# Score matmuls of 48 and 49 rows in two halves of the partitions, with the heads of a pair stacked above each other

## The reference

```
D = E // H                      # 16 numbers a head
qh = q.reshape(B, S, KV, G, D).transpose(0, 2, 3, 1, 4)
kh = k.reshape(B, S, KV, D).transpose(0, 2, 1, 3)
scores = einsum('bkgsd,bktd->bkgst', qh, kh) / 4
weights = softmax(scores, axis=-1)
out = einsum('bkgst,bktd->bkgsd', weights, vh)
```

## Time and profile before

| | us |
|---|---|
| median of 3 runs | 2073.77 |
| range of the runs | 2072.3 to 2074.99 |
| span of the profiled execution | 2071.6 |
| VectorE busy in the span | 1417.0 (68%) |
| TensorE busy in the span | 1536.0 (74%) |
| ScalarE busy in the span | 717.8 (35%) |

### The profile page before, as it was taken

How to read it: one execution, slowest core, us unless ns; L and a number is a source line. 1 busy time by engine, 2 the same in 40 slices (tenths; PEclk the granted TensorE clock), 3 DMA queues, 4 the chain that set the end, 5 groups by cost and what they waited for, 6 DMA issues and landing times.

```text
span 2071.6 us, 25320 instructions
## 1 busy us (share of the span) xinstructions
PE 1536.0 (74%) x8378; PEld 759.6 (37%) x8379; DVE 1417.0 (68%) x2322; ACT 717.8 (35%) x976; POOL 414.0 (20%) x318
## 2 busy tenths in 40 slices
PE   2121313069993899992589888898889999999997
PEld 1111212046662566661122222222234444444443
DVE  7999999963336222227988787888656777777765
ACT  2134342521122233333166565665612222222221
POOL 3054443410000111115200000000022222222222
PEclk7565655579996999996599999999989999999999
DMA  5223231310013122225502011020300000000000
GB/s 185 81 102 125 85 96 64 124 44 24 20 48 103 61 81 81 81 76 145 170 1 39 14 21 32 0 46 21 130 13 1 0 20 0 20 0 0 20 0 21
DMA packets 54861, 113.90 MB, mean 55 GB/s; under 512 B 8520, under 2 KB 24136, under 8 KB 51728
## 3 DMA queue, kind: packets, MB, share of 16 engines
q1 hardware_dynamic: 49040, 94.29, 14.2%
q0 software_dynamic: 5760, 18.88, 3.4%
HBM read 72.11 MB, written 31.46 MB: 50 GB/s over the span
## 4 chain that ended last, share of the span: by engine, by line
PE 39%; DVE 29%; issue 19%; POOL 7%; ACT 3%; DMA 2%; DVEq 0%; SPq 0%; POOLq 0%; ACTq 0%
PE PS L635 13%; PE PS L650 7%; PE PS L1360 5%; DVE WORK L1485 5%; PE PS L1339 5%; DVE BIG L1659 4%; POOL BIG L1664 3%; PE PS L1348 3%; DVE BIG L1658 2%; DVE BIG L1660 2%; POOL BIG L1668 2%; ACT BIG L1672 2%; PE PS L625 1%; DVE WORK L1658 1%; DMA WORK<-in_L_ffn_w_dram 1%
## 5 line engine op out<-in xcount | busy, mean ns | idle before, releaser
L1485 DVE TENSOR_REDUCE WORK<-PS 128x1 f32<-128x512 f32 x512 | 326.3, 685 | 71.3 <-PE PS L1339 68.4
L1870 PE MATMUL PS<-BIG 128*128 128x512 f16 x1536 | 339.8, 383 | 8.6 <-DVE BIG L1941 6.8
L1267 ACT ACTIVATE BIG<-PS 128x1024 f32<-128x1024 f32 x256 | 261.5, 1024 | 165.8 <-PE PS L1348 164.6
L635 PE MATMUL PS<-BIG,WORK 128*128 (+1 forms) x1728 | 273.7, 316 | 5.1 <-DVE WORK L670 4.7
L1339 PE MATMUL PS<-BIG 128*128 128x512 f16 x512 | 205.6, 404 | 68.9 <-DVE WORK L1485 45.1
L1870 PEld LDWEIGHTS PS<-BIG 128*128 128x128 f16 x1536 | 151.3, 99 | 194.4 <-issue 14.3
L635 PEld LDWEIGHTS PS<-BIG,WORK 128*128 128x128 f16 x1728 | 168.1, 99 | 97.7 <-issue 12.7
L1893 PE MATMUL PS<-BIG 128*128 128x512 f16 x768 | 175.7, 382 | 16.3 <-DVE BIG L1965 16.3
L674 DVE SCALAR_TENSOR_TENSOR WORK<-PS,WORK 128x352 f32<-128x352 f32 x72 | 37.7, 524 | 211.7 <-ACT WORK L662 211.7
L1348 PE MATMUL PS<-BIG 128*128 128x512 f16 x512 | 155.2, 387 | 0.1
L650 PE MATMUL PS<-BIG,WORK 128*128 (+1 forms) x648 | 151.7, 379 | 3.8 <-DVE WORK L679 3.8
(11 more groups left out here) (225 smaller groups left out, 2265.2 us busy)
## 6 DMA issues: line engine op xcount, KB each, us to landing
wdq_scratch<-BIG SPq DMA_DIRECT2D x12, 1024.0 KB, 4.8
BIG<-wdq_scratch SPq DMA_DIRECT2D x12, 1024.0 KB, 6.1
WORK<-in_L_ffn_w_dram SPq DMA_DIRECT2D x32, 352.0 KB, 3.8
y_scratch<-WORK SPq DMA_DIRECT2D x40, 256.0 KB, 2.5
BIG<-BIG SPq DMA_DIRECT2D x96, 64.0 KB, 2.3
BIG<-in_L_ffn_gate_w_dram SPq DMA_DIRECT2D x4, 1024.0 KB, 6.3
BIG<-in_L_ffn_up_w_dram SPq DMA_DIRECT2D x4, 1024.0 KB, 7.4
X<-in_x_dram SPq DMA_DIRECT2D x4, 1024.0 KB, 14.0
```

Of the source, the lines that this page charges most:

```text
L635: ins = nc.tensor.matmul(bank[1 + 2 * m + up][:, 0:I], xT[:, p, a, k * P:(k + 1) * P], W13[:, bass.ds(slot * W13N + (w * half + k * 2 * I ...
L1267: nc.scalar.activation(PB[:, tp, 2 * h:2 * h + 2, :], BPAIR[h % 2], ACT.Exp, scale=SOFT_SCALE).then_inc(exp_ok, 1)
L1485: v.tensor_reduce(MXU[:, g % 2, c:c + 1], ABANK[i], AX_X, ALU.max, negate=True).then_inc(max_ok, 1)
L1870: ins = nc.tensor.matmul(bank[b], fxT[:, p, a, k * P:(k + 1) * P], w[:, c, l, k, :], start=(i == 0), stop=(i == 3 * KD - 1))
```

## The change

Two heads of a group now stand in the two halves of the partitions: the 48 rows of the even heads in 0 to 47, those of the odd heads in 64 to 111. QS has half as many columns (H/2 instead of H heads), and KK is written to both halves, in one copy instead of two. The maxima go to rows 48 and 112, in two DMAs. An A matmul uses 48 rows of one half, a B matmul 49. Each is issued as a matmul on 64 of the array's 128 rows: rows 0 to 63 or rows 64 to 127. The order in a slot is A (lower half), B (upper), B (lower), A (upper). B matmuls signal one by one. The stacking of one group takes 12 DMAs instead of 6. The clearing of the unused rows goes: VectorE, GpSimd and ScalarE cleared whole ranges before the stage, and VectorE wrote the row of ones (L1559); now GpSimd and VectorE fill 32 rows of KK each with ones. The order of the UW weight loads at the end of the stage is another, as the columns come free in another order.

```diff
-                    sp.dma_start(QS[rows, g * HG:(g + 1) * HG, :], qhT[g * HD:(g + 1) * HD, a, :, :]).then_inc(qk_in[g], 16)
-                    sp.dma_start(KK[rows, g, :, :], khT[g * HD:(g + 1) * HD, w, :].unsqueeze(1).to_broadcast([HD, 2, S])
-                                 ).then_inc(qk_in[g], 16)
+                    for i in range(2):
+                        rows = slice(64 * i + n * HD, 64 * i + (n + 1) * HD)
+                        sp.dma_start(QS[rows, g * HP:(g + 1) * HP, :], heads[g * HD:(g + 1) * HD, a, :, i, :]
+                                     ).then_inc(qk_in[g], 16)
+                        sp.dma_start(KK[rows, g, :], khT[g * HD:(g + 1) * HD, w, :]).then_inc(qk_in[g], 16)
...
-                sp.dma_start(QS[64:65, g * HG:(g + 1) * HG, :].rearrange("o h (r s) -> o (h r) s", r=R),
-                             MT[:, i, :]).then_inc(m_in[i], 16)
+                for half in range(2):
+                    row = 64 * half + ROWS
+                    sp.dma_start(QS[row:row + 1, g * HP:(g + 1) * HP, :].rearrange("o h (r s) -> o (h r) s", r=R),
+                                 MT[half * HP * R:(half + 1) * HP * R, i, :]).then_inc(m_in[i], 16)
...
-                    r = 2 * tp + i
-                    nc.tensor.matmul(ABANK[i], QS[:, g * HG + h, r * P:(r + 1) * P], KA[:, g, :],
+                    r = 2 * tp + h // 2
+                    rows = slice(64 * i, 64 * i + ROWS)
+                    nc.tensor.matmul(ABANK[i], QS[rows, g * HP + h % 2, r * P:(r + 1) * P], KK[rows, g, :],
                                      start=True, stop=True).then_inc(a_mm, 1)
...
-                for j in range(HALF):
-                    t = HALF * tp + j
-                    ins = nc.tensor.matmul(BPAIR[h % 2][:, j, :], KS[:, g, t * P:(t + 1) * P],
-                                           QS[:, g * HG + h, :], start=True, stop=True)
-                ins.then_inc(b_mm, 1)
+                t = HALF * tp + h // 2
+                for i in (1, 0):
+                    rows = slice(64 * i, 64 * i + ROWS + 1)
+                    nc.tensor.matmul(BPAIR[h % 2][:, i, :], KK[rows, g, t * P:(t + 1) * P],
+                                     QS[rows, g * HP + h % 2, :], start=True, stop=True).then_inc(b_mm, 1)
...
-            link(v.memset(QS.rearrange("p a b -> p (a b)")[32:64, :].bitcast(F32), 0.0))
+            v.memset(KK.rearrange("p a b -> p (a b)")[96:128, :].bitcast(F32), ONE_ONE).then_inc(ones_ok, 1)
...
-            v.memset(KS[64:65, :, :], 1.0).then_inc(cpad_ok, 1)
```

More of the change, by code:

```diff
@@ L1 @@
+import struct
 from contextlib import ExitStack
@@ L739, in b_gpsimd @@
             pool.wait_ge(MO.y_mm, SLOTS)
[L740 removed]
+            nc.gpsimd.memset(KK.rearrange("p a b -> p (a b)")[32:64, :].bitcast(F32), ONE_ONE).then_inc(ones_ok, 1)
             for p in range(2):
@@ L1085, in build @@
         HG = H // G
[L1086 to L1089, removed]
+        HP = HG // 2
+        ROWS = 3 * HD
+        QS = carve(BIG, "QS", 0, [P, H // 2, S], F16)
+        KK = carve(BIG, "KK", 32768, [P, G, S], F16)
+        ONE_ONE = struct.unpack("<f", struct.pack("<I", 0x3C003C00))[0]
         PB = carve(BIG, "PB", 49152, [P, 2, 2 * HG, S])
@@ L1108, in build @@
         ct_in = sem("ct_in")
-        cpad_ok = sem("cpad_ok")
-        zeros_ok = sem("zeros_ok")
+        ones_ok = sem("ones_ok")
         row_st = sem("row_st")
@@ L1162, in stack_group @@
             def stack_group(b, g):
+                heads = qhT.rearrange("p a (h i) s -> p a h i s", i=2)
                 for n, (a, w) in enumerate(((0, 0), (0, 1), (1, 0))):
-                    rows = slice(n * HD, (n + 1) * HD)
-                    sp.dma_start(QS[rows, g * HG:(g + 1) * HG, :], qhT[g * HD:(g + 1) * HD, a, :, :]).then_inc(qk_in[g], 16)
-                    sp.dma_start(KK[rows, g, :, :], khT[g * HD:(g + 1) * HD, w, :].unsqueeze(1).to_broadcast([HD, 2, S])
-                                 ).then_inc(qk_in[g], 16)
+                    for i in range(2):
[3 more added lines that the diff above has]
+                        sp.dma_start(KK[rows, g, :], khT[g * HD:(g + 1) * HD, w, :]).then_inc(qk_in[g], 16)
             def maxima(u, g, i):
                 sp.wait_ge(mt_ok, u + 1)
-                sp.dma_start(QS[64:65, g * HG:(g + 1) * HG, :].rearrange("o h (r s) -> o (h r) s", r=R),
-                             MT[:, i, :]).then_inc(m_in[i], 16)
+                for half in range(2):
+                    row = 64 * half + ROWS
+                    sp.dma_start(QS[row:row + 1, g * HP:(g + 1) * HP, :].rearrange("o h (r s) -> o (h r) s", r=R),
+                                 MT[half * HP * R:(half + 1) * HP * R, i, :]).then_inc(m_in[i], 16)
             def batch(b, last):
@@ L1183, in batch @@
                         maxima(u + 1, (g + 1) % G, (g + 1) % 2)
[L1184 to L1188, removed]
+                    if last and g == 2:
+                        load_weights(UW, 1, 2, uw_in)
+                    if last and g == 4:
+                        sp.wait_ge(b_mm, u * 4 * HG)
+                        load_weights(UW, 1, 0, uw_in)
+                    if last and g == 6:
+                        load_weights(UW, 1, 3, uw_in)
                     if last or g < 5:
@@ L1193, in batch @@
                     for gg in {5: (0, 1, 2, 3), 6: (4, 5), 7: (6,)}[g]:
-                        sp.wait_ge(b_mm, (b * G + gg + 1) * 2 * HG)
+                        sp.wait_ge(b_mm, (b * G + gg + 1) * 4 * HG)
                         stack_group(b + 1, gg)
                 if not last:
-                    sp.wait_ge(b_mm, (b * G + G) * 2 * HG)
+                    sp.wait_ge(b_mm, (b * G + G) * 4 * HG)
                     stack_group(b + 1, G - 1)
@@ L1204, in c_sync @@
             load_ctx(0)
-            sp.wait_ge(cpad_ok, 1)
+            sp.wait_ge(ones_ok, 2)
             sp.wait_ge(t_free, tuse(None, "q", R - 1) + 1)
@@ L1215, in c_sync @@
             batch(B - 1, True)
-            sp.wait_ge(b_mm, B * G * 2 * HG)
-            load_weights(UW, 1, FCH - 1, uw_in)
+            sp.wait_ge(b_mm, B * G * 4 * HG)
+            load_weights(UW, 1, 1, uw_in)
             sp.wait_ge(pv_mm, B * G * 2)
@@ L1265, in batch @@
                         for h in range(HG):
-                            act.wait_ge(b_mm, n * HG + (h + 1))
+                            act.wait_ge(b_mm, n * (2 * HG) + 2 * (h + 1))
                             nc.scalar.activation(PB[:, tp, 2 * h:2 * h + 2, :], BPAIR[h % 2], ACT.Exp,
@@ L1283, in c_scalar @@
             act.wait_ge(MO.y_mm, SLOTS)
[L1284 to L1287, removed]
             nc.scalar.nop().then_inc(exp_ok, 2)
@@ L1359, in pv @@
                 for h in range(HG):
-                    ins = nc.tensor.matmul(OBANK[32 * h:32 * h + 32, :], V[:, t, g, :], PB[:, tp, 2 * h + j, :],
+                    ins = nc.tensor.matmul(OBANK[32 * h:32 * h + 32, :], V[:, t, g, :], PB[:, tp, HG * j + h, :],
                                            start=(t == 0), stop=(t == R - 1))
@@ L1370, in batch @@
                         if tp == 0:
-                            pe.wait_ge(m_in[g % 2], (u - g % 2) * 8 + 16)
+                            pe.wait_ge(m_in[g % 2], (u - g % 2) * 16 + 32)
                         ahead = not (last and g >= G - 2)
@@ L1483, in max_slot @@
                     dve.wait_ge(a_mm, n + 1)
-                    c = h * R + 2 * tp + i
+                    c = i * HP * R + h % 2 * R + 2 * tp + h // 2
                     v.tensor_reduce(MXU[:, g % 2, c:c + 1], ABANK[i], AX_X, ALU.max, negate=True).then_inc(max_ok, 1)
```

9 lines of the change are left out of this document (3 added, 6 removed).

## The result

| | before | after |
|---|---|---|
| median, us | 2074.38 (4 runs, 2072.3 to 2075.64) | 2181.2 (4 runs, 2172.56 to 2183.26) |
| span of the profiled execution | 2071.6 | 2178.3 |
| TensorE clock over the span | 0.872 | 0.826 |

The account below looks back on a forecast made before the run. Bound by the turn between TensorE and VectorE, neither full, with SyncE's queue as third party. 2071.6 + 20.9 prologue + 54.3 boundaries + 3 clock - 7.5 overlap = 2142.3; median 2.2 higher, 2144.5 us, range 2105 to 2158.

Parts of the forecast that it names:

- the clock's 3: TensorE behind long stalls at the three batch boundaries: half clock for a few us, 1 us each, 3 us lost.
- The issue doesn't shrink with the size: SyncE's stacking DMAs: half-size transfers keep the present issue pitch, about 0.655 us, 0.685 in the prologue.
- rival (a): SyncE's queue: issue time goes with size, pitch 0.33 us, nothing stalls, 2065 us; chance 0.05.
- rival (b): SyncE's queue: small transfers issue somewhat faster, at 0.545 us, 2107 us; chance 0.20.
- the prologue: Start of the stage: 96 stacking DMAs instead of 48 delay unit 0's first maxima, costing 20.9 us.
- The stalls: Three batch boundaries: TensorE waits for SyncE's transfers before groups 6, 7 and next group 0, not group 1; 18.1 us each.
- the queue's terms: SyncE's doubled issues at the start and three batch boundaries: 20.9 us plus 54.3 us lost.
- The halves overlap: TensorE's A and B matmuls in alternating halves run side by side: 0.27 us a unit, 7.5 us gained in all.
- rival (c): TensorE's score matmuls: the halves don't overlap, no 7.5 us gained, 2152 us, or 2158 with pitch 0.685; chance 0.15.
- The drain between tilings: TensorE's tiling mode changes: some 0.1 us each, 6 to 10 us if all on the chain; put at 0.

Follow-up runs that it names:

- queue-only kernel: Kernel before, full 128-row matmuls, with every stacking DMA and the maxima's DMA split in two; 2146.3 us, ratio 1.0358.
- experiment 6: Changed kernel with every score matmul on all 64 rows of its half, the added rows zeros against ones; 2151.36 us, ratio 1.0381.
- Experiment 3: Changed kernel with every B matmul issued twice, 2166.54 us; also with SyncE's transfers spread, 2103.73; then context load moved, B twice only in groups 0 to 4, 2101.7.
- experiment 7: Changed kernel, KK stacking by GpSimd, all 64 rows: 2074.66 us; plus B twice in groups 0 to 4: 2078.08; control, kernel before with spread transfers: 2072.99.
- experiment 5: Kernel before with score matmuls on 48 or 49 rows of one half, one after the other, on 64 array rows; 2305.46 us, ratio 1.1133.

## Why the prediction was wrong, point by point

Distances between the maxima's transposes (of units counted from 0), each less that of before, in us; 1 is the queue-only kernel, 6 the one on 64 rows:

| stretch | predicted | after | 1 | 6 |
|---|---|---|---|---|
| start to unit 0 | 20.9 | 17.0 | 18.4 | 18.5 |
| units 0 to 5 | -1.4 | 9.3 | 0.1 | 1.2 |
| boundary, 5 to 9 | 18.6 | 22.5 | 19.7 | 21.8 |
| units 9 to 13 | -1.1 | 8.2 | 0.1 | -0.4 |
| boundary, 13 to 17 | 18.6 | 20.9 | 16.5 | 18.3 |
| units 17 to 21 | -1.1 | 8.1 | -0.1 | 0.5 |
| boundary, 21 to 25 | 18.6 | 23.6 | 17.6 | 20.5 |
| units 25 to 30 | -2.4 | 0.0 | -0.1 | -1.8 |

The predicted column shares out the 70.7 us of the sum, with the clock's 3 in the boundaries (18.1 + 1 less 0.5 for two units). The after column sums to 109.6; the span grew by 106.7, so 2.9 are gained outside these stretches. Of the 36.7 us between the forecast and the result, the clock is most (below).

**The issue doesn't shrink with the size: right.** 591 and 627 ns against the earlier trace rows; rival (a) would have had 0.33 us, rival (b) 0.545. The prologue's pitch was 0.661 (0.685 taken) and the first issue came 1.05 us earlier, so the first slot of unit 0 starts at 1045.19 and not at 1048.4, and the prologue cost 17.0, not 20.9; the boundaries' pitch was 0.671 ((1167.75 - 1135.55) / 48), not 0.655.

**The stalls: right in size, not in every place.** At the first boundary TensorE waits 3.04 us before group 6 for a stack (3.7 forecast) and 11.49 before group 7 (some 11 named). Before the next group 0 it waits 1.43 and not 3 to 4, for group 7 had run in part at half clock and ended later. Before group 1 it waits 5.97 where the forecast had "no further stall"; the queue-only kernel waits 3.88 there, so this slip is not the clock's. In that kernel the start and the three boundaries cost 72.2 us together (18.4 + 19.7 + 16.5 + 17.6), where 20.9 + 54.3 = 75.2 were forecast, and 78.2 with the clock's 3: the queue's terms hold, and the clock behind stalls alone was not put too low.

**The halves overlap: right.** 13.33 us a unit; rival (c) falls. Units with the transposes of q, 14.61 us before, take 14.20 where the clock holds (experiment 6), so these gain 0.4 and not 0.27. The drain between tilings, put at 0, has no visible price: the chain is as forecast, and from the last A matmul to the PV block it is 0.31 us (1545.38 to 1545.69) as before.

**The clock, "behind long stalls the clock is at half for a few us: 1 us each, 3": this step failed.** The sum took the full clock of the earlier trace rows as given for the new matmuls, and charged only the stalls. The fewer rows also take from TensorE what kept its clock up: it ran at half clock in large parts of units that wait for no transfer. That the halved time does so too fits experiments 3 and 6, but no run isolates it. Experiment 6 measures the term by giving the rows back: 2181.2 - 2151.4 = 29.8 us instead of 3, and rather more, since its own clock is not full everywhere. Without it the forecast is 2141.5, and 2151.4 was measured. By the table, the boundaries are 7.8 of the difference (60.6 against 52.8 without the clock) and the units between them 5.5 (-0.5 against -6.0, for the first units of a batch are still at a clock share below 1 in experiment 6), less 2.4 in the prologue; that is 10.9 for a difference of 9.9, and the rest is rounding and what lies outside the table's stretches.

**What is shown and what is open.** Rows were changed both ways, and the clock moved with them each time. From 48 or 49 to 64 in each half, nothing else in the form of the matmuls changed (experiment 6, faster by 30, and in experiment 7 faster by 35). From 128 to 48 or 49 (experiment 5, slower by 233), the part of the array that a matmul is issued on went from 128 rows to 64 as well; how much of the 233 is due to that, no run shows. Experiment 3 moved the clock with more work on the same rows. Not settled: whether rows of zeros count as much as rows of data (they do count), why the last batch of the changed kernel keeps the full clock with the same forms of matmuls, and why three or four units of experiment 5 do.

## What to carry to other kernels

- Before matmuls are made narrower in rows, read the granted clock of the stage, and price the stage at both clocks: at 1.2 GHz the PV block cost 1.86 instead of 0.99 us. If the clock falls, fill the rows: on a half's 64 rows the matmuls cost no time more than on 48 (13.33 us a unit both times), and zeros in one of the two operands were enough here.
- A queue that binds nothing has slack, not no cost: count its issues (0.59 to 0.63 us each on SyncE, from 2 KB to 64 KB) between two transfers that somebody waits for. Moving half of them to GpSimd, with the rows filled, brought the changed kernel from 2181 to 2075, level with before. Its units away from the boundaries do gain what the halves gave (most take 14.20 and 13.33 us against 14.61 and 13.61), but its start costs 3.5 us more, and in the first units of a batch the clock is still not full.

## What the runs showed of the hardware that was not expected

- TensorE busy 50.00 of 50 us at a granted clock of 0.50 (matmuls on 48 or 49 rows), and at 1.00 when busy 44.52 of 50 (128 rows).
- Zeros (against ones) in otherwise unused rows raised the clock of a stretch from 0.76 to 0.94 and from 0.80 to 0.98.
- Issuing work twice made a kernel faster, by 15 to 23 us in three pairs of runs (2181.2 to 2166.5, 2121.8 to 2103.7, 2109.3 to 2086.4). With the rows filled it did not (2074.7 to 2078.1).
